# Token rows kept in one SBUF tile through all nine stages, and another order of work at the heads and tails of the attention stages

## The reference, cut to what matters

```python
x = x + tanh(g_xattn[0]) * attention16(layernorm(x), ctx)        # stage l0x, 16 heads of 16, 77 context keys
x = x + tanh(g_ffn[0])   * light_and_routed_heavy_ffn(layernorm(x))      # l0f
x = x + tanh(g_xattn[1]) * perceiver64(ctx, layernorm(x))        # l1x, 16 heads of 64, 1024 + 77 keys, layer norm on the output
x = x + tanh(g_ffn[1])   * bitlinear_conv_ffn(layernorm(x))      # l1f
x = x + tanh(g_xattn[2]) * attention16(layernorm(x), ctx)        # l2x
x = x + tanh(g_ffn[2])   * top2_of_8_experts(layernorm(x))       # l2f
x = x + tanh(g_xattn[3]) * perceiver64(ctx, layernorm(x), rms)   # l3x, 4 heads of 64, rms norm of q and k
x = x + tanh(g_ffn[3])   * block(layernorm(x))                   # block(h): y = h + self_attention16(ln(h)) (l3a); y + top1_of_8_experts(ln(y)) (l3f)
```

## Time and profile before

| | us |
|---|---|
| median of three runs (3599.72 to 3605.78) | 3603.96 |
| the profiled execution | 3608.14 |
| its span, first to last instruction | 3606.4 |
| PE / DVE / ACT / POOL busy in it | 3055.0 / 1659.4 / 1326.0 / 1270.4 |

### The profile page before, as it was taken

The page is one execution under the profiler, slowest core; times in us unless marked ns, Lnnn a source line. Parts: engine busy times, 40 slices in busy tenths (PEclk is TensorE's granted clock), DMA queues, the critical chain, the costliest instruction groups (busy, mean ns, idle before and its releaser), DMA issues. The chain is left out here.

```text
span 3606.4 us, 42616 instructions
## 1 busy us (share of the span) xinstructions
PE 3055.0 (85%) x15849; PEld 1669.9 (46%) x15849; DVE 1659.4 (46%) x3210; ACT 1326.0 (37%) x1792; POOL 1270.4 (35%) x1020
## 2 busy tenths in 40 slices
PE   7888799999999995868759999838985899985796
PEld 3455334444344432433548888713432223223685
DVE  3535455646455462665511111235554777773001
ACT  3332344343434432454212221114442565552231
POOL 2241266656656565202241111324573210001212
PEclk8989899999999997978779999968998999997898
DMA  3101100000000001020144444420001000002444
GB/s 116 49 30 41 41 5 10 5 5 10 5 10 5 17 1 50 9 72 7 42 168 181 184 163 166 150 84 5 7 6 56 1 1 7 7 1 84 170 175 137
DMA packets 94409, 205.62 MB, mean 57 GB/s; under 512 B 9773, under 2 KB 72162, under 8 KB 81444
## 3 DMA queue, kind: packets, MB, share of 16 engines
q0 software_dynamic: 20352, 122.43, 9.0%
q1 hardware_dynamic: 73892, 80.96, 7.0%
HBM read 162.21 MB, written 41.16 MB: 56 GB/s over the span
## 5 line engine op out<-in xcount | busy, mean ns | idle before, releaser
L1500 POOL TENSOR_TENSOR l1x_added<-l1x_added,l1x_probs 128x1024 f32<-128x1024 f32 x224 | 527.3, 2354 | 264.4 <-ACT l1x_probs L1758 198.5
L1856 DVE TENSOR_REDUCE l1x_tops<-l1x_ring 128x1 f32<-128x512 f32 x512 | 326.7, 685 | 208.6 <-PE l1x_ring L1575 207.8
L1118 DVE TENSOR_REDUCE l3a_halves<-l3a_ring 128x1 f32<-128x512 f32 x512 | 324.3, 683 | 105.6 <-PE l3a_ring L962 103.0
L1758 ACT ACTIVATE l1x_probs<-l1x_slots 128x1024 f32<-128x1024 f32 x256 | 262.0, 1024 | 239.3 <-PE l1x_slots L1615 237.5
L1608 PE MATMUL l1x_slots<-l1x_Q,l1x_K 64*128 64x512 f32 x1152 | 310.8, 617 | 7.4 <-ACT l1x_probs L1756 4.8
L1078 ACT ACTIVATE l3a_probs<-l3a_slots 128x1024 f32<-128x1024 f32 x256 | 248.1, 1021 | 160.7 <-PE l3a_slots L982 160.7
L1630 PE MATMUL l1x_pv<-l1x_probs,l1x_V 128*64 128x512 f32 x1152 | 285.6, 611 | 5.2 <-ACT l1x_probs L1756 5.2
L3193 ACT ACTIVATE l2f_sg<-l2f_hid 128x256 f32<-128x256 f32 x184 | 70.7, 384 | 386.2 <-PE l2f_hid L3126 386.2
L3333 DVE TENSOR_TENSOR l2f_hh<-l2f_sg,l2f_hid 128x256 f32<-128x256 f32 x184 | 77.5, 421 | 275.4 <-ACT l2f_sg L3193 275.4
L3126 PE MATMUL l2f_hid<-l2f_xgT,l2f_gate 128*128 128x256 f32 x736 | 190.5, 381 | 1.1 <-ACT l2f_xgT L3182 1.1
L3126 PE MATMUL l2f_hid<-l2f_xgT,l2f_up 128*128 128x256 f32 x736 | 189.8, 380 | 0.0
(11 more groups left out here) (669 smaller groups left out, 5290.0 us busy)
## 6 DMA issues: line engine op xcount, KB each, us to landing
l1x_w<-in_l_qkv SPq DMA_DIRECT2D x16, 384.0 KB, 3.1
slots_in<-zeros POOLq DMA_DIRECT2D x1, 5888.0 KB, 27.1
l2f_xg<-slots_in SPq DMA_DIRECT2D x23, 256.0 KB, 2.9
slots_out<-l2f_y SPq DMA_DIRECT2D x23, 256.0 KB, 2.2
l3f_xg<-slots_in SPq DMA_DIRECT2D x15, 256.0 KB, 3.1
slots_out<-l3f_y SPq DMA_DIRECT2D x15, 256.0 KB, 2.2
l0x_x<-in_x SPq DMA_DIRECT2D x4, 512.0 KB, 16.5
x<-l0x_x SPq DMA_DIRECT2D x4, 512.0 KB, 2.9
```

Of the source, the lines that this page charges most:

```text
L1118: nc.vector.tensor_reduce(halves[:, k % 2, col:col + 1], bank_of(banks[e]), AX.X, ALU.max).then_inc(s["bank_done"], 1)
L1500: ins = nc.gpsimd.tensor_tensor(added[h][:], added[h][:], probs[:, n % PROBS, :, :], ALU.add)
L1758: ins = nc.scalar.activation(p, s2[m % 2], ACT.Exp)
L1856: ins = nc.vector.tensor_reduce(tops[:, e * NT + t, h:h + 1], bank, AX.X, ALU.max)
```

## The change

**One tile for the rows.** `c.x` is allocated once; the stages use it. The rows are loaded once, in l0x. No stage but l3f stores its result at its end, and no `wait` on stores holds the barrier. The one exception is a copy of l3x's result to DRAM (`x6`, the base of l3f): SP issues the four copies as the chunks are ready, but only POOL in l3a (before it overwrites the first chunk) and SP in l3f wait for them, on a semaphore that the stages don't clear. The weight loads that stood behind the `x` loads on SP's queue move up; in cross16 `wq` also moves ahead of `wv`.

**Order.** In `plan_cross` the norm is applied and transposed first, then context keys; a value job stands behind each of the first two queries, and the maxima are shifted. In `plan_self` the chunk 0 transposes stand ahead of norm 1, and one piece of a projection (four matmuls) follows each of the 16 steps of maxima. In `plan64` without rms one value tile ("early", four matmuls) follows each of the first seven steps, and the evacuation writes the bf16 copy first; with rms the value job moves between "root" and "low". `close(2)` in the tail moves behind the last sums.

```diff
+    c.x = sb("x", [P, TT, D])
+    c.base_stored = nc.alloc_semaphore("base_stored")
...                                                    (plan_cross)
-    events.append(("norm", 0))
+    events += [("norm", 0), ("apply", 0)]
+    for k in range(KD):
+        job("xt", 0, k, pool=slots)
     job("kc", 0, 3, pool=slots)
     job("kc", 3, 4, pool=slots)
     events.append(("keys",))
-    for b in range(B):
-        job("vc", b, pool=slots)
-    events.append(("apply", 0))
-    for k in range(KD):
-        job("xt", 0, k, pool=slots)
     for u in range(3):
         query(u, pool=slots)
         if u < 2:
+            job("vc", u, pool=slots)
+        if u:
+            maxima(u - 1, 1)
+        if u < 2:
             maxima(u, 0)
-            maxima(u, 1)
     turn(0)
...                                                    (SP in cross16; the same edit in every stage)
-            load_x(0)
+            if x_in is not None:
+                load_x(0)
...
-            for n in range(NC):
-                sp.wait_ge(s["out_added"], (n + 1) * CT)
-                sp.dma_start(tiles_of(x_out, n * CH, CT), x[:, n * CT:(n + 1) * CT, :]).then_inc(s["stored"], 16)
-            sp.wait_ge(s["stored"], 16 * NC)
...                                                    (plan_self)
-    events += [("norm", 0), ("norm", 1)]
+    events.append(("norm", 0))
     for k in range(KD):
         job("xt", 0, k, pool=slots)
+    events.append(("norm", 1))
...
+    pieces = [("v", 0, i, 1) for i in range(NT)] + [("q", 0, CH + i, 256) for i in (0, 256)] + [("k", 1, i * 256, 256) for i in range(4)] + [("q", 1, i, 256) for i in (0, 256)]
+    for k, e in zip(order, pieces):
         maxima(0, [k])
-        if n in (1, 3, 5, 7):
-            job("v", 0, n - 1, 2, pool=slots)
...
+        job(*e, pool=slots)
+        if e[0] != "v" and e[2] % CH:
+            low(e[0], e[1], e[2] // CH)
...                                                    (POOL in self16: V's memset behind norm 1; ahead of the first overwriting of x:)
+                if n == 0:
+                    pool.wait_ge(c.base_stored, 16 * NC)
...                                                    (plan64)
     if rms:
-        events += [("root", None, 0), ("low", None, 0)]
+        events.append(("root", None, 0))
+        job("v", 0)
+        events.append(("low", None, 0))
     waiting += steps(0, range(0, 4), (0, 4)) + steps(0, range(4, NT), (4, NT))
-    maxima(4)
-    job("v", 0)
-    maxima(8)
+    if rms:
+        maxima(12)
+    else:
+        for t in range(NT):
+            maxima(1)
+            if t < NT - 1:
+                events.append(("early", slot, 0, t))
+        job("v", 0)
+        maxima(4)
     turn(1)
...
-                    close(*last)
+                    if last != (phases - 1, 0):
+                        close(*last)
...
     sums(*end)
+    close(phases - 1, 0)
     job("wo", *end)
     close(*end)
...                                                    (PE in cross64)
+            def value_tile(out, at, t):
+                b, wi = at // PAIRS, w[at % 2]
+                for k in range(KD):
+                    last = nc.tensor.matmul(out[:, t * P:(t + 1) * P], lT[:, k, b * S + t * P:b * S + (t + 1) * P], wi[:, 2, k, :],
+                                            start=k == 0, stop=k == KD - 1)
+                return last
...
+                elif e[0] == "early":
+                    value_tile(slot_free(pe, e[1]), *e[2:])
...                                                    (ACT in cross64, and the same for k)
-                    nc.scalar.activation(Q[i][:], ps, ACT.Copy, scale=0.125).then_inc(s["q_ready"], 1)
-                    ins = nc.scalar.activation(Qb[i][:], ps, ACT.Copy, scale=0.125)
+                    nc.scalar.activation(Qb[i][:], ps, ACT.Copy, scale=0.125).then_inc(s["qb_ready"], 1)
+                    ins = nc.scalar.activation(Q[i][:], ps, ACT.Copy, scale=0.125)
...                                                    (SP in moe, l3f only)
             if base is not None:
+                sp.wait_ge(c.base_stored, 16 * NC)
                 sp.dma_start(base_sb[:], tiles_of(base, 0, TT)).then_inc(s["base_loaded"], 16)
```

More of the change, by code:

```diff
@@ L264, in plan_cross, with cross16 @@
     return events
-def cross16(nc, c, name, x_in, x_out, w, gate, ctx_t, mask=None, slots_out=None):
+def cross16(nc, c, name, x_in, w, gate, ctx_t, mask=None, slots_out=None):
     QUADS, PROBS, QS = 4, 2, 4
@@ L578, in norm @@
             def norm(n):
-                dve.wait_ge(x_loaded[n], 16)
+                if x_in is not None:
+                    dve.wait_ge(x_loaded[n], 16)
                 if n:
@@ L1404, in _ @@
             load_w(1)
-            for n in range(2, NC):
-                load_x(n)
             for at in range(2, U):
@@ L1409, in _ @@
                 load_w(at)
-            for n in range(NC):
-                sp.wait_ge(out_ready[n], 1)
-                sp.dma_start(tiles_of(x_out, n * CH, CT), x[:, n * CT:(n + 1) * CT, :]).then_inc(s["stored"], 16)
-            sp.wait_ge(s["stored"], 16 * NC)
+            if x_copy is not None:
+                for n in range(NC):
+                    sp.wait_ge(out_ready[n], 1)
+                    sp.dma_start(tiles_of(x_copy, n * CH, CT), x[:, n * CT:(n + 1) * CT, :]).then_inc(c.base_stored, 16)
         @block.gpsimd
@@ L3013, in _ @@
                 store(v * SLOTS, v % 2)
-            for n in range(NC):
-                sp.wait_ge(s["out_ready"], n + 1)
-                sp.dma_start(tiles_of(x_out, n * CH, CT), x[:, n * CT:(n + 1) * CT, :]).then_inc(s["stored"], 16)
-            sp.wait_ge(s["stored"], 16 * NC)
+            if x_out is not None:
+                for n in range(NC):
+                    sp.wait_ge(s["out_ready"], n + 1)
+                    sp.dma_start(tiles_of(x_out, n * CH, CT), x[:, n * CT:(n + 1) * CT, :]).then_inc(s["stored"], 16)
+                sp.wait_ge(s["stored"], 16 * NC)
         @block.gpsimd
@@ L3426 @@
     io["out"] = nc.dram_tensor("out_0", (TOK, D), F32, kind="ExternalOutput").ap()
[L3427 to L3428 removed]
+    io["x6"] = nc.dram_tensor("x_6", (TOK, D), F32, kind="Internal").ap()
     program(nc, io)
@@ L3442, in program @@
         io["scratch"] = nc.dram_tensor("scratch", (TT, P), F32, kind="Internal").ap()
[L3443 removed]
+        cross16(nc, c, "l0x", io["x"], weights(io, "l0x"), 0, io["ctx_t"], mask=io["mask0"], slots_out=io["slots_in"])
         c.end_stage()
[L3445 removed]
+        ffn0(nc, c, "l0f", 4, io)
         c.end_stage()
[L3447 removed]
+        cross64(nc, c, "l1x", io["l1_qkv"], io["l1_wo"], 1, io["ctx"], io["mask1"], io["mask1_t"], io["l1_ln"],
                     out_ln=(io["l1_go"], io["l1_bo"]))
         c.end_stage()
[L3450 removed]
+        ffn1(nc, c, "l1f", 5, io)
         c.end_stage()
[L3452 removed]
+        cross16(nc, c, "l2x", None, weights(io, "l2x"), 2, io["ctx_t"])
         c.end_stage()
[L3454 removed]
+        moe(nc, c, "l2f", None, 6, 2, io, weights(io, "l2e"))
         c.end_stage()
[L3456 to L3457 removed]
+        cross64(nc, c, "l3x", io["l3_qkv"], io["l3_wo"], 3, io["ctx"], io["mask3"], io["mask3_t"], io["l3_ln"],
+                    rms=io["l3_gam"], out_b=io["l3_bo"], x_copy=io["x6"])
         c.end_stage()
[L3459 removed]
+        self16(nc, c, "l3a", weights(io, "l3a"), io["l3_ln1"])
         c.end_stage()
[L3461 removed]
+        moe(nc, c, "l3f", io["out"], 7, 1, io, weights(io, "l3e"), io["l3_ln2"], io["x6"])
         c.end_stage()
```

143 lines of the change are left out of this document (37 added, 106 removed).

## The result

The changed kernel takes 3508.57 us (median of four runs, 3500.58 to 3509.64) against 3604.87 for the kernel before in the same session. The ratio on record is 0.9717, 95% interval 0.9699 to 0.9736 (the quotient of the two medians, 0.9733, lies inside it). In a second session it was 3509.89 against 3608.48, ratio 0.9734 (0.9712 to 0.9756). The forecast of 3514 lies 4 to 5 us above, inside its range.

The account below looks back on a forecast made before the run. PE bounds the loops, so the gains lie in idle time at boundaries, heads and l1x's tail. Boundaries 48.4, heads 34.7 and tails 7.0 sum to 90.1 us: 3608.1 becomes 3518 profiled, 3514 as median; range 3500 to 3540.

Parts of the forecast that it names:

- The boundary: Between stages: without row stores and loads, DVE idles 1.3 us instead of about 8; all eight boundaries save 48.4 us.
- Boundaries: 6.3 with the store: Start of l3x: gam lands 7.6 us after the new start instead of 10.8, saving 6.3 us with the store.
- Heads: Stage starts up to first scores: l2x 7.0, l0x 8.1, l1x 6.2, l3x 3.5, l3a 9.9; together 34.7 us saved.
- ACT's evacuation: l3x's head: evacuating the moved value job ahead of the bf16 copies delays the maxima, losing 1.7 us.
- the two terms 5.5 and 1.0: l1x's head: 5.5 us saved by spreading value tiles between maxima, 1.0 by making the bf16 copy first.
- the 3.8 us ahead of the maxima: l3a's head: transposes ahead of norm 1 and V's later memset bring the first maxima 3.8 us earlier.
- The term of 6.1 in the maxima: l3a's head: a projection piece behind each step of maxima saves 6.1 us over 16 steps.
- Tails: Stage ends: l1x saves 6.5 us by moving close(2) behind the last sums, l3x 0.5; together 7.0.
- It is wrong if a loop's length changes: Sign of failure: the prediction is wrong if a loop's length changes or a head waits for a weight.
- Rival 4: Loops: denser TensorE work makes the chip grant less clock, so slower than before, 3640 us; chance 0.02.
- Rival 2: New heads: the clock stays at 1.2 GHz, losing about 29 us in all, 3543 us; chance 0.09.
- Rival 1: Stage heads: other loads of weights and constants are late, giving back 11 to 20 us, 3530 us; chance 0.14.

Follow-up runs that it names:

- 3: Changed kernel with SP storing the rows again at stage ends and waiting for the stores before the barrier, no loads; 3534.65 us.
- the repeat: The changed kernel measured and profiled once more, unedited; 3509.89 us.
- 4: Changed kernel with three extra copies nobody reads on DVE at the end of l2f; 3509.72 us, ratio 0.9730.
- 5: Changed kernel with l1x's and l3x's value jobs back among the maxima (l1x's a block) and close(2) ahead of the last sums; 3528.02 us, ratio 0.9767.
- 6: Changed kernel with cross64's float copy of q and k first, and l3a's norms both ahead of chunk 0's transposes; 3514.67 us, ratio 0.9731.
- run 8: Changed kernel with unread TensorE matmuls at the start of every stage and ahead of the experts in l2f and l3f; 3507.44 us, ratio 0.9714.
- 2: Kernel before with only the new orders of work, rows still stored and loaded at every boundary; 3559.30 us, ratio 0.9869.
- 9: Changed kernel with the three moves of 7 and 12 unread matmuls at the start of six stages; 3493.23 us, ratio 0.9682.
- 1: Changed kernel with all orders of work as in the kernel before, only the rows kept in one tile; 3559.18 us, ratio 0.9873.
- 7: Changed kernel with gam's scaling later in l3x, an addition of close(2) on DVE, and l1f's chunk 1 statistics before the w1 sum; 3504.47 us, ratio 0.9703.
- the repeat of the kernel before: The kernel before measured and profiled once more, unedited; 3608.34 us.

## Why the prediction was right, and where it was not

**The total.** The terms that the sum had gave 88.6 us for 90.1. Single terms missed by up to 3.3 us, in both directions; that they nearly cancel is luck. Two of the sums were slips: l1x's head adds up to 6.0 and not 6.2, l3x's to 3.4 and not 3.5. The 9.8 us outside the sum are a miss of mechanism, told below.

**The boundary.** Right, and shown by 3: the store costs 3.0 us, the load the rest, the barrier 1.2. Six of eight terms are within 0.3 us; l1x's was 1.2 too small: `cx` alone landed 2.7 us after its issue, where I had taken the `x` chunk's 3.8. There the rule of the Trainium skill that I had set beside the trace ("DMA: Bandwidth & Descriptors", anatomy of one DMA), with its 2.4 us, was nearer than my row. The section gives that rule for DMAs that GpSimd issues, and these loads are SP's. In l1f the 1 MB of `w1` took 5.1 us, as I had put it, and not the 4.4 that the rule gives.

**l3x's boundary.** The step "Boundaries: 6.3 with the store" failed: 3.0. The load of `gam` was sized well enough (6.9 us from the stage's start, forecast 7.6, 7.5 in the repeat), but the start itself did not come nearer to DVE's last operation (4.65 us before, 5.51 after), as there POOL and not the store had held the barrier, before as after (4).

**Heads.** Terms within 1.3 us but l2x, where 9.3 came for 7.0: keys took 3.77 for 4.4 and the query jobs 1.88 from the first on. In l3x ACT's evacuation cost the bf16 copies 0.4 us and not 1.7, and the value job ran at full clock (3.84). In l1x the two terms 5.5 and 1.0 did not hold alone: undone, they cost 2.9 and nothing (5, 6). The 5.5 was a block mostly at half clock; the 1.0 was there at the first maxima and lost again to the clock of the last steps. That the head still gave 5.4 I put down to the clock; no run takes that apart. In l3a the 3.8 us ahead of the maxima came (4.0, 3.2 in the repeat), but mostly not from the transposes (0.3 to 1.1, run 6). The term of 6.1 in the maxima was too large: 4.8, at 1.38 us a step and not 1.29.

**Tails.** 6.3 in place of 7.0; undoing it cost 7.2 together with what the clock did in that profile. POOL's two operations over 1024 columns (a multiplication and an addition, not two additions) stood ahead of its part of `close(3)` as forecast, which began at 1387.01 with its statistics ready since 1384.0.

**Everything else, 9.8 for 0.** The prediction put what lies behind the heads at nothing and named its own sign of failure, "It is wrong if a loop's length changes". Loops did change, in l2x and l2f with TensorE's clock. 3.4 us in l2x and the 4.5 in l2f (3.2 of them by the end of the routing) belong to the program: both executions of the one kernel have them, neither of the other. So does l0x's 1.5: behind its first scores it took 117.7 us in all three profiles with the old order, 114.6 or 116.2 in the ten with the new. The rest, l3f among it, is within what one program does from one execution to the next. Rival 4 did not come: of what follows the heads only l1f got longer by more than 0.4 us (1.1), and the mean granted clock rose from 0.921 to 0.934. Something of its kind shows in one place alone, l2x in run 8, for 2.4 us.

**Rival 2.** Out: in the new heads TensorE was granted full clock (1.13 us a piece of four in l3a, 0.71 a value tile in l1x). Where only bf16 products stand between waits the clock can be low: l3x's maxima take 0.61 us for 0.39, at 0.50 in this window of the changed kernel (columns as above), and l1x's last steps likewise.

```profile
2350.00:2356.00 6.00, 2.73 (x18) 0.78 (x16) 5.32 (x9) 0.00 (x0) 0.00 (x0) 0.50 0.00 0
```

It costs little: eight such steps take DVE 11.09 us, where four at full clock take 4.87 (run 5). In l3x the trace agrees with the rule of the Trainium skill as I had set it beside this rival ("TensorE: Matmul & The Clock Gate", HAM oscillation). That section speaks of waits for DMAs; here the waits are for a PSUM bank, 0.79 us each. But the rule does not decide the level: products with the same waits kept full clock (0.39) in most steps of l1x in the kernel before, and in its last steps in runs 2, 6, 8 and 9. Where pieces of a projection stand between the products, no fall showed.

**Rival 1.** Out: of the loads only `gam`, `w1` and `cx` set the length of a head, as forecast.

**Not settled.** What decides the level in l2f's head. It was not the gap ahead alone: the boundary was 7.91 us long in run 2 and 4.57 in run 3, and the copy behind the routing came at 32.1 and 35.2 us. That either half of the change by itself takes away l2x's fall says only that it hangs on where the stage's work falls, not on one edit.

## What to carry to other kernels

Keep data that the next stage needs where it is, and then look which engine holds each barrier: seven of eight were held by a store, and the eighth by the engine that issues indirect DMAs, where dropping the store gained nothing. Price a block of matmuls at the clock it will have after the change, not at the one in the profile before, if the change also removes the gaps ahead of it. Before a term under some 5 us of a stage is believed, profile the same kernel twice.

## What the runs showed of the hardware

- TensorE's clock differs between executions of one program: the head of l0x took 33.0 and 27.5 us, its key jobs 1.40 and 0.79. In both, the granted clock of that stretch is given as 1.00; at the start of a profile only the lengths tell. That one program meets either level fits what the Trainium skill says of the clock gate's window ("TensorE: Matmul & The Clock Gate", Part 1: The HAM clock gate): it runs freely and does not restart with the kernel. No run here shows the window itself.
- The heads of the two expert stages come in steps: the first copy behind the routing stands near 35, 32 or 29 us behind the norm. Seen in l2f: 35.2 in the kernel before twice and in 3, 32.1 in the changed kernel twice and in 1, 2, 4, 5, 6 and 7; in l3f 35.0 nearly always, 31.9 in the repeat of the kernel before, 29.2 and 29.0 in 1 and 2. With matmuls at the start (8 and 9) it is 30.7 in l2f and 33.7 in l3f.
- With 12 matmuls that nobody reads at the start of a stage, the heads of l1x, l2x, l2f and l3a were 1.3 to 2.3 us shorter (l1x's was as short in run 2 without them); where the rest of the stage then fell back (l2x) nothing was left.
- The stage behind l2f began 9.0 us after POOL's last issue of an indirect DMA in all 13 profiles (8.98 to 9.03), whether a store was waited for (run 3) or DVE had more to do (run 4).
